# The expert layer's weighted sum: eight VectorE instructions against eight ScalarE instructions and two accumulating DMAs

## The reference

```python
out = jnp.zeros_like(xf)
for e in range(E):
    h = jax.nn.silu(xf @ w1s[e])
    out = out + combine[:, e:e + 1] * (h @ w2s[e])
...
def step(h, ins):
    d_t, B_t, C_t, u_t = ins
    dA = jnp.exp(d_t[:, :, None] * A)
    h = h * dA + (d_t * u_t)[:, :, None] * B_t[:, None, :]
    y = jnp.einsum('bds,bs->bd', h, C_t)
...
x = x + 0.5 * _L0_ffn_ref(_layernorm(x, axis=-1), ...)
x = x + _L0_attn_ref(_layernorm(x, axis=-1), ...)
x = x + 0.5 * _L0_ffn_ref(_layernorm(x, axis=-1), ...)
```

## Time and profile before

| | before |
|---|---|
| median of 3 runs | 1673.58 us (1672.91 to 1674.64) |
| the profiled execution | 1679.97 us, its span 1678.1 us |
| VectorE busy in the span | 1391.7 us (83%) |
| ScalarE busy | 1278.2 us (76%) |
| TensorE busy | 1327.8 us (79%) |
| GpSimd busy | 650.4 us (39%) |

### The profile page before, as it was taken

The page is one execution under the profiler, slowest core; times in us unless marked ns, Lnnn a source line. Parts: engine busy times, 40 slices in busy tenths (PEclk is TensorE's granted clock), DMA queues, the critical chain, the costliest instruction groups (busy, mean ns, idle before and its releaser), DMA issues. The chain is left out here.

```text
span 1678.1 us, 29290 instructions
## 1 busy us (share of the span) xinstructions
PE 1327.8 (79%) x8754; PEld 1191.0 (71%) x8754; DVE 1391.7 (83%) x2149; ACT 1278.2 (76%) x2660; POOL 650.4 (39%) x681
## 2 busy tenths in 40 slices
PE   7978567878888787888878788877878787668778
PEld 6867456767777686777767687776867676457668
DVE  3367989989899888989889898989899888978742
ACT  3489658978788788979889797978889698548722
POOL 1212434263624536263523536263533534242220
PEclk9989769989989799988999899998999899768889
DMA  6336346676666667665666767665675765464631
GB/s 198 110 88 141 79 81 153 144 169 133 157 133 136 147 140 177 144 162 122 143 152 137 163 140 178 142 160 115 146 162 130 165 145 104 82 137 106 156 90 45
DMA packets 144231, 227.04 MB, mean 135 GB/s; under 512 B 13648, under 2 KB 79440, under 8 KB 143952
## 3 DMA queue, kind: packets, MB, share of 16 engines
q0 software_dynamic: 39424, 123.76, 37.8%
q1 hardware_dynamic: 104656, 101.41, 21.0%
HBM read 90.90 MB, written 25.17 MB: 69 GB/s over the span
## 5 line engine op out<-in xcount | busy, mean ns | idle before, releaser
L977 ACT ACTIVATE dA<-delta,A 128x255 f32<-128x255 f32 x1024 | 425.7, 495 | 5.3 <-DVE hs L1345 4.4
L1351 DVE TENSOR_TENSOR_SCAN hs<-dA,b_r 128x512 f32<-128x512 f32 x256 | 297.6, 1202 | 17.2 <-PE b_r L664 12.3
L1345 DVE TENSOR_TENSOR_SCAN hs<-dA,dbu 128x1024 f32<-128x1024 f32 x128 | 292.7, 2287 | 16.6 <-ACT dA L977 10.2
L539 PE MATMUL b_h<-xsT,wst 128*128 128x128 f32 x1680 | 253.7, 299 | 35.4 <-issue 28.6
L539 PEld LDWEIGHTS b_h<-xsT,wst 128*128 128x128 f32 x1680 | 227.2, 209 | 55.3 <-issue 53.4
L1363 DVE TENSOR_TENSOR G<-hs,b_r 128x1024 f32<-128x1024 f32 x192 | 233.3, 1215 | 33.1 <-PE b_r L675 27.6
L551 PE MATMUL b_out<-w2s,hT 128*128 x1680 | 234.8, 286 | 11.0 <-ACT ys L898 9.2
L847 ACT ACT_TABLE_LOAD x182 | 233.5, 1283 | 3.9 <-PEq L1751 0.7
L551 PEld LDWEIGHTS b_out<-w2s,hT 128*128 128x128 f32 x1680 | 215.8, 200 | 16.3 <-issue 14.8
L664 PE MATMUL b_r<-prm,scaled 128*128 128x128 f32 x1024 | 173.6, 300 | 57.0 <-ACT scaled L993 28.8
L993 ACT ACTIVATE scaled<-duT,dtT 128x256 f32<-128x256 f32 x512 | 217.0, 500 | 1.4 <-PE b_r L664 1.1
(11 more groups left out here) (179 smaller groups left out, 2256.1 us busy)
## 6 DMA issues: line engine op xcount, KB each, us to landing
wst<-w_dram SPq DMA_DIRECT2D x242, 256.0 KB
acc<-G POOLq DMA_DIRECT2D x96, 512.0 KB
odd<-G POOLq DMA_DIRECT2D x96, 512.0 KB
xsort<-sorted SPq DMA_DIRECT2D x70, 192.0 KB
results<-ys SPq DMA_DIRECT2D x70, 192.0 KB, 3.1
odd<-xd POOLq DMA_DIRECT2D x32, 256.0 KB
xin<-x_dram SPq DMA_DIRECT2D x8, 256.0 KB
sorted<-ys SPq DMA_DIRECT2D x2, 960.0 KB, 7.5
```

Of the source, the lines that this page charges most:

```text
L539: last = mm(H[r % 2][:, w], wst[k % NW][:, w], xsT[i // CH % 2][:, t:t + P], start=True, stop=True)
L977: last = do(dA[j % 4][:, d, k, 1:], delta[b][:, k, 1:], ACT.Exp, scale=A[:, k, s:s + 1])
L1345: V.tensor_tensor_scan(flat(hs[j % 2]), flat(dA[j % 4]), flat(dbu[n % 2]), 0.0, ALU.mult, ALU.add)\
L1351: V.tensor_tensor_scan(hs[j % 2][:, d, :, :].rearrange("p h t -> p (h t)"), dA[j % 4][:, d, :, :].rearrange("p h t -> p (h t)"), R[u % 2][ ...
```

## The change

VectorE's `fsum` is gone. In slots 0 and 2, ScalarE multiplies the eight gathered tiles by their weights where they lie (`fw`, the new function `ffn_weigh`), and GpSimd issues two DMAs of 256 KB that add the halves of `yk` to the sum (`fa0`, `fa1`, the new function `ffn_add`); the second is issued when the first has landed. The new semaphore `f_sum` counts their landings; whoever waited for `f_yacc` waits for it. `lx`, `ln` and `unx` stand later in slot 2, and `lx` waits for `f_sum`; on GpSimd `lnx` and `rmsx` stand behind `a4`. The semaphore `f_sum` reaches its value in slot 0 or 2; `f_yacc` had it at the end of slot 3 or 1. After the last slot both steps of layer 14 stand at the head of `finish`.

```diff
 "scalar": (
-        "d0 e1 d1 d2 F0 e3 d3 F1 F2 e5 F3 r xm d4 proj d5 sp F4 F5 e7 F6 oT dx F7 d6 d7 v F8 rT",
+        "d0 e1 d1 fw d2 F0 e3 d3 F1 F2 e5 F3 r xm d4 proj d5 sp F4 F5 e7 F6 oT dx F7 d6 d7 v F8 rT",
...
-        "d0 e1 F0 d1 F1 F2 e3 F3 e5 F4 d2 d3 d4 d5 d6 turned d7 e7 F5 F6 r xm F7 proj F8 sp F9 F10 F11 dx",
+        "d0 e1 F0 d1 F1 F2 e3 F3 e5 F4 fw d2 d3 d4 d5 d6 turned d7 e7 F5 F6 r xm F7 proj F8 sp F9 F10 F11 dx",
...
 "vector": (
...
-        "b0 fstats s0 s1 g0 fnorm b2 s2 flog ftop g1 fplace gate g2 s3 b4 xsum g3 un s4 g4 s5 g5 b6 fweights s6 g6 low s7 delta g7 fsum",
-        "b0 s0 s1 g0 gate b2 g1 xsum s2 s3 un g2 b4 lx g3 s4 s5 g4 ln b6 low s6 g5 unx delta g6 s7 g7",
-        "b0 fstats s0 s1 fnorm b2 g0 flog ftop g1 fplace s2 g2 s3 gate g3 b4 s4 fweights g4 s5 low g5 b6 delta s6 mask g6 s7 g7 xb fsum",
+        "b0 fstats s0 s1 g0 fnorm b2 s2 flog ftop g1 fplace gate g2 s3 b4 xsum g3 un s4 g4 s5 g5 b6 fweights s6 g6 low s7 delta g7",
+        "b0 s0 s1 g0 gate b2 g1 xsum s2 s3 un g2 b4 g3 s4 lx s5 g4 b6 low s6 ln g5 delta g6 unx s7 g7",
+        "b0 fstats s0 s1 fnorm b2 g0 flog ftop g1 fplace s2 g2 s3 gate g3 b4 s4 fweights g4 s5 low g5 b6 delta s6 mask g6 s7 g7 xb",
...
 "gpsimd": (
-        "skip a2 a3 a4 a5 a6 a7",
+        "skip a2 fa0 a3 fa1 a4 a5 a6 a7",
...
-        "skip rms rs a2 a3 lnx rmsx a4 a5 a6 a7",
+        "skip rms rs a2 fa0 a3 fa1 a4 lnx rmsx a5 a6 a7",
...
+        def ended(g):
+            return second(g - 2) if g >= 2 else None
...
             def store(g):
-                sp.wait_ge(f_yacc, second(g))
+                sp.wait_ge(f_sum, 32 * second(g))
                 sp.dma_start(ot[g], ob[:, :, :]).then_inc(s_store, 16)
...
             def whole_turned(n, tiles=slice(0, TILES)):
...
                 if n:
-                    act.wait_ge(f_yacc, SORTED)
+                    act.wait_ge(f_sum, 32 * SORTED)
...
+            def ffn_weigh(n):
+
+                act.wait_ge(s_gat, 16 * 2 * TILES * n)
+                act.wait_ge(f_weights, 2 * n + 2)
+                for k in range(2):
+                    for j in range(TILES):
+                        last = do(yk[:, k, j, :], yk[:, k, j, :], ACT.Identity, scale=c01[n % 2][:, k, j:j + 1])
+                last.then_inc(f_weighed, 1)
...
             def ffn_weights(f, t=slice(0, TILES)):
 
                 dve.wait_ge(f_th, f[0] + 1)
+                wait(dve, f_weighed, min(f[0], LAST) - 2)
...
-            def ffn_sum(f):
-
-                n, src, dst, g, is_first = f
-                dve.wait_ge(s_gat, 16 * 2 * TILES * n)
-                dve.wait_ge(f_weights, 2 * n + 2)
-                dve.wait_ge(f_keep, n + 1)
-                for k in range(2):
-                    for j in range(TILES):
-                        last = V.scalar_tensor_tensor(
-                            out=dst[:, j, :], in0=yk[:, k, j, :], scalar=c01[n % 2][:, k, j:j + 1], in1=dst[:, j, :],
-                            op0=ALU.mult, op1=ALU.add)
-                    if not k:
-                        dve.drain()
-                last.then_inc(f_yacc, 1)
...
                             if name == "lx":
+                                dve.wait_ge(f_sum, 32 * first(nxt))
                                 mixer_norm_stats(nxt)
...
             def ffn_gather(n, x):
...
-                    wait(pool, f_yacc, m)
+                    wait(pool, f_sum, 32 * m)
...
+            def ffn_add(f, k):
+
+                n, dst = f[0], f[2]
+                if k == 0:
+                    pool.wait_ge(f_weighed, n)
+                    pool.wait_ge(f_keep, n + 1)
+                else:
+                    pool.wait_ge(f_sum, 32 * (n - 1) + 16)
+                Q.dma_start(dst[:, :, :], yk[:, k, :, :], accum_op=ALU.add).then_inc(f_sum, 16)
...
             def finish():
                 one, two = slice(0, HALF), slice(HALF, TILES)
                 f = (LAST, xb, ob, GROUPS - 1, False)
+                last = (second(GROUPS - 2), xb, ob, GROUPS - 2, False)
+                ffn_add(last, 0)
+                ffn_add(last, 1)
                 ffn_root(LAST, one)
```

More of the change, by code:

```diff
@@ L299, in moe_mamba_kernel @@
             sem("f_mask"), sem("f_weights"), sem("f_count"), sem("f_pos"), sem("f_tile"), sem("f_keep"))
-        f_hmm, f_hact, f_ymm, f_ys, f_yacc = (
-            sem("f_hmm"), sem("f_hact"), sem("f_ymm"), sem("f_ys"), sem("f_yacc"))
+        f_hmm, f_hact, f_ymm, f_ys, f_weighed, f_sum = (
+            sem("f_hmm"), sem("f_hact"), sem("f_ymm"), sem("f_ys"), sem("f_weighed"), sem("f_sum"))
         d_up, d_act, d_y, d_sum = sem("d_up"), sem("d_act"), sem("d_y"), sem("d_sum")
@@ L1006, in memory_reads, with slot @@
                 do(rT[:, :], W[0][:, 0:T], ACT.Copy).then_inc(g_r, 1)
-            def slot(g, i, tail, head, n, nx):
+            def slot(g, i, tail, head, n, nx, done):
                 for name, num in steps("scalar", i):
@@ L1018, in slot @@
                             ffn_leave(n, num)
+                    elif name == "fw":
+                        if done is not None:
+                            ffn_weigh(done)
                     elif name == "ftanh":
@@ L1054, in finish @@
                 tail = (GROUPS - 1, 1)
+                ffn_weigh(second(GROUPS - 2))
                 whole_turned(LAST, slice(0, HALF))
@@ L1074, in run @@
                     head = (g, i + 1) if i < 3 else None if is_last else (g + 1, 0)
-                    slot(g, i, tail, head, (n1, n2)[i // 2], (n2, n3)[i // 2])
+                    slot(g, i, tail, head, (n1, n2)[i // 2], (n2, n3)[i // 2], (ended(g), n1)[i // 2])
             start()
@@ L1414, in slot @@
                         scan_output(g, i, num)
-                    elif name == "fsum":
-                        if f:
-                            ffn_sum(f)
                     elif name in next_steps:
@@ L1627, in residual, with slot @@
                 Q.tensor_tensor(rs[:, tiles, :], xam[:, tiles, :], x1[:, tiles, :], ALU.add).then_inc(g_rs, 1)
-            def slot(g, i, tail, head, f, fx, nxt):
+            def slot(g, i, tail, head, f, fx, nxt, done):
                 for name, num in steps("gpsimd", i):
@@ L1640, in slot @@
                             ffn_gather(f[0], num)
+                    elif name == "fa":
+                        if done:
+                            ffn_add(done, num)
                     elif name == "fkeep":
@@ L1683, in run @@
                 f3 = n3 is not None and (n3, xin, xa, g + 2, True)
+                f0 = ended(g) is not None and (ended(g), xb, ob, g - 2, False)
                 for i in range(4):
@@ L1686, in run @@
                     head = (g, i + 1) if i < 3 else None if is_last else (g + 1, 0)
-                    slot(g, i, tail, head, (f1, f2)[i // 2], (f2, f3)[i // 2], None if is_last else g + 1)
+                    slot(g, i, tail, head, (f1, f2)[i // 2], (f2, f3)[i // 2], None if is_last else g + 1, (f0, f1)[i // 2])
             start()
```

## The result

The changed kernel took 1760.79 us (median of 4 runs, 1759.93 to 1762.23). Beside 1674.11 us of the kernel before on the same chip that is a ratio of 1.0503, with a 95% interval of 1.0482 to 1.0524: 5% slower, some 87 us, where I had said 41. (By the ratio it is 84 us, and that figure is used from here on.) The direction was right; the time is above the range.

A forecast was written before the change was run, and what follows sets the result against it. VectorE was taken to set the pace of the slots, with ScalarE close behind; -11.8 + 39.9 + 26.0 - 5.3 + 4.7 - 12.0 = +41.5 us on the 1673.6 us median gave 1715 us, 8-in-10 range 1676 to 1745.

The forecast's parts named there:

- Removed: the sums: On VectorE, 14 sums and the idle time before them, 70.3 us, go; twelve of them are 5.3 us each.
- Added: the weighing on ScalarE: ScalarE's 2.4 us of weighing leaves slot 2 gaining 1.5 us in six groups, 2.8 in group 0: -11.8 us.
- `finish`: After the last slot, ScalarE's copy into `yk` waits for layer 14's additions: +4.7 us, bounds +3 and +6.
- `ln` behind `s6` costs nothing: In slot 2, VectorE's b6 and s6 take about as long as GpSimd's a4 and root, so no cost.
- The new wait on VectorE: In slot 2, `lx` waits 5.7 us for both additions to land, in seven groups: +39.9 us.
- taken back: Short waits later in the pair go, 1 us for each of the 12 new waits: -12.0 us.
- The new wait on SyncE: In slot 0 the store waits for `fa1`, delaying the weight load, U4 and `b6`: +5.2 us in five groups, +26.0.
- Group 0: Its first sum, 2.8 us of work, is gained whole in slot 2; its `lx` waits 5.7 us like the others.
- the hold hidden: Rival: SyncE's hold doesn't reach TensorE, as U4's buffer is filled in time; +10 us, 1684 us, chance 0.10.
- no line at the DMA engines: Rival: additions land 3.0 us after issue, not queued behind `a3`; +11.5 us, 1685 us, chance 0.08.
- ScalarE in time: Rival: ScalarE isn't late, VectorE gains the sums whole, both new waits stand; -2 us, 1671 us, chance 0.04.
- The faster one: Rival: additions have landed when asked for, so neither `lx` nor U4 waits; -18 us, 1656 us, chance 0.12.

The follow-up runs named there:

- e3: The changed kernel with SyncE's store behind tile 9's weight load and the additions of slots 2 and 0 issued earlier on GpSimd; ratio 1.0054 to the kernel before.
- e6: The kernel before, its sums still on VectorE but moved to early in slots 2 and 0, store behind tile 9's weight load; ratio 1.0007.
- e12: The kernel before with only the store moved behind the weight load of tile 9, as a control; ratio 1.0000.
- e5: e3 with ScalarE weighing one column in place of eight tiles, so the computation leaves the weighing out; ratio 0.9903 to the kernel before.
- e8: The kernel before with only lx, ln and unx later in slot 2, and GpSimd's lnx and rmsx behind a4; ratio 1.0024.
- e1: The changed kernel with SyncE's store moved behind the weight load of tile 9; ratio 1.0236 to the kernel before.
- e4: The kernel before, with SyncE's store in groups 2 to 6 also waiting until addition a3 of slot 0 has landed; ratio 1.0258.
- e7: e3 with GpSimd weighing the eight tiles directly before the first addition, instead of ScalarE; ratio 1.0024 to the kernel before.
- e9: The kernel before with only second layers' sums (slot 0) the new way, weighed by GpSimd, additions before a2 and a3, store late; ratio 0.9937.
- e10: e9 with ScalarE weighing instead of GpSimd, at the changed kernel's place in slot 0; ratio 1.0010 to the kernel before.

## Why the prediction was wrong

Both new waits came where they were forecast, and so did `s2`'s wait for its decays. What failed is the sum of everything else, and the size of the hold on SyncE; together they are the missing 43 us.

- **"Removed: the sums" and "Added: the weighing on ScalarE"** (-11.8, -1.1 five times, -5.3; with `finish` -17.9 us): measured +9.0, so 27 us are missing here. This is the step that failed most: that VectorE, with the sums gone, would be 3.4 us earlier in slot 2, of which the weighing leaves 1.0 to 1.5.
  - From the end of slot 1's last product to `acc`'s product behind `s1`, VectorE took 11.0 us before and takes 9.3 in e3 (means of groups 2 to 6). So 1.7 us are gained there, not 3.4. e6 shows the reason: the wait for the gathers was cover for `d0`, `d1` and the first banks. I had looked at the distance to `d1`'s end alone, and not at the other things that VectorE asks for in the first 10 us of the slot, when it arrives there 5 us earlier: the bank of `b0`, `d0`, and the bank that TensorE makes behind `d1`.
  - Then come waits that the kernel before hardly had, in e3 1.8 us at `s2` for the decays behind `fw`, 0.6 at `g3` and 0.9 at `b6` for banks (the same means). At the slot's end nothing is left: slots 1 and 2 together take 99.0 us in e3, against 97.1 before and 96.9 in e12. Without the weighing they take 96.0 (e5): a gain of about 1, not 3.4, and the weighing's 2.4 us cost 3.0.
  - In slot 0 VectorE does arrive 5.0 us earlier, and is still 1.9 earlier at `g3` in e3 (forecast 1.1); but slots 3 and 0 together gain 1.5 us beside before and 0.2 beside e12, so whether the 1.1 held isn't shown. Slot 3 of group 6 and slot 0 of group 7, where the forecast was 5.3, gained 3.1 (84.5 us after, 87.6 before) and 3.9 in e3.
- **"`ln` behind `s6` costs nothing"**: it costs 4.0 us (e8), a part of the 27.
- **"The new wait on VectorE"**: idle for 42.1 us, forecast 39.9; worth 32. So some 10 us are **taken back**, 1.4 for each of seven; the forecast had 1.0.
- **"The new wait on SyncE"**: forecast 26.0 with it and -5.5 without it, a swing of 31.5, of which 5.0 were to be taken back; measured 43. In group 3 the store was released 7.8 us after `g3`, not 6.1 (`a3` and `fa1` were issued 0.5 us apart, and `a4` at 712.21 came beside them); the load took 4.5, not 4.0; and from U4 to `b6` it took 5.1 us, not 3.2, at half the clock. I had named the clock as the upper bound of this term, and taken the lower value. Over groups 2 to 6, beside e1: `b6` begins 9.6 us later after `g3` (forecast 6.3), `g3` itself 0.7 later, and 1.7 are taken back behind `b6`, where slot 0 ends 9.9 us after it instead of 11.6. That is 8.6 us for each of five, 43.
- **`finish`**: forecast +4.7; from the last slot's first `dbu` (1555.81 us before, 1632.81 after) to the span's end it grew by 5.3 us. The number held in part by luck, for the root behind both additions wasn't in it.
- **Group 0**: its slots took 9.3 us more, forecast 2.9: `lx` waited 7.3 us there, and the sum's 2.8 us weren't gained at all.

So the rest is 27 us above the forecast, the hold 16.5 (43 against 31.5 - 5.0), and `lx` 1 below it (32 against 39.9 - 7.0): 42.5 us, and 84.2 - 41.5 = 42.7. The rivals: the hold hidden and no line at the DMA engines are out by e1 to e4 and the timelines. ScalarE in time is out by e5: even without the weighing only 16 us are gained. The faster one was in fact built as e3, in which the additions have landed when they are asked for, and it gave +9.0, not -18.

**The page's price of a DMA.** In group 2 `fa1` landed 4.0 us after its issue (612.27 to 616.25), and part 6 has medians of 5.0 and 5.4. In that time `a3` landed too, and the DMA engines were at a share of 1.04:

```profile
612.20:615.50 3.30, 3.15 (x26) 2.85 (x24) 0.00 (x0) 1.95 (x5) 0.87 (x1) 1.00 1.04 190
```

That is 190 GB/s; the earlier trace rows had 184 at a share of 0.96. The nearest to an addition alone is the second of `finish`, 3.3 us. The Trainium skill's page "DMA: Bandwidth & Descriptors", section "Anatomy of one DMA — SWDGE (gpsimd) path", would have 2.6 us and 436 GB/s; the trace doesn't agree, and the measurement decides. (The prediction priced the page's case twice and differently: 29 us below its sum, and 1677 us, which is 38 below it. Its rival's terms give the second.)

## What to carry to other kernels

Idle time before an instruction can't simply be taken: move the instruction first (e6, two lines of a table) and see what waits in its stead, before you pay another engine for its work. A new wait on a queue costs what stands behind it in that queue: find what TensorE needs from there, and put the waiting instruction behind it (43 us for the store's place, and nothing measurable when it is late, e12). And the halves of a change can have opposite signs: with GpSimd weighing, slots 3 and 0 gained and slots 1 and 2 lost (e7), and the kernel with only the first half (e9) is the fastest that computes everything. The same half with ScalarE weighing (e10) gains nothing.

## What the runs showed of the hardware

**GpSimd's elementwise work made VectorE's longer.** In e7, slot 2 of group 2, the timeline of VectorE, and of GpSimd beside it:

```profile
580.05 2.23 DVE L1293 SCALAR_TENSOR_TENSOR varr<-mvr 128x1 f32<-128x1 f32 x2
```

```profile
579.69 5.12 POOL L1579 TENSOR_SCALAR yk<-yk,c 128x128 f32<-128x128 f32 x8
```

Two operations on one column took 2.23 us, in the kernel before 0.35. Over the program `varr` goes from 297 to 534 ns, and VectorE is busy for 23.0 us more than in e5, beside 69.4 us of weighing on GpSimd. The groups of the even scans in e5 and in e7, by line and form:

```profile
L1344 DVE TENSOR_TENSOR_SCAN hs<-dA,dbu 128x1024 f32<-128x1024 f32 x128 | 294.2, 2299 | 17.8 <-ACT dA L986 12.7 <-issue 0.2
```

```profile
L1346 DVE TENSOR_TENSOR_SCAN hs<-dA,dbu 128x1024 f32<-128x1024 f32 x128 | 306.5, 2395 | 17.4 <-ACT dA L989 12.1 <-issue 0.2
```

These scans, whose two inputs `dA` and `dbu` both lie in SBUF (the memory on the chip that holds the kernel's tiles), are busy 12.3 us longer, `varr` 7.4 and `un<-x` 3.5: that is the whole 23. The odd scans and the products, which read one input from TensorE's bank, stay at 299.2 and some 233.5 us. The Trainium skill's page "SBUF — State Buffer", section "SBUF: two separate sides", says that VectorE and GpSimd share one pair of ports, which whoever comes first holds for a whole instruction, so that the other stands still; it counts VectorE's operations with two inputs in SBUF among those. The rows agree in kind; for `un<-x`, with one input tensor, the quoted case doesn't speak. That is a part of why e7 isn't e5; how large a part I didn't measure.

**TensorE's clock behind a wait.** Idle before U4, TensorE had a granted clock of 0.54 in the last 4.5 us of it and of 0.50 in the 5.1 us of work behind it. In e4 the same U4 took 2.07 us behind 9.13 us of waiting. Over the program the granted clock fell from 0.904 to 0.874 with the change.

**Two accumulating DMAs in a row are slow for their size.** 256 KB within SBUF took 4.0 to 6.9 us from issue to landing beside others (`fa1` of group 2, `fa1` of slot 0 of group 3) and 3.3 nearly alone, and eight ScalarE instructions of 128 columns took 2.44 us, as estimated (2.4): a sum that VectorE forms in 2.35 to 2.8 us took 10.8 us from gathers to landing in `finish`.
